# Score matmuls of causal cross-attention, 128 keys at a time, issued as four column groups of 32 keys

## What is computed

```python
def _L0_xattn_ref(x, mem, Wq, Wkv, Wout, bout):
    q = x @ Wq
    kv = jnp.concatenate((mem, x), axis=1) @ Wkv
    k, v = jnp.split(kv, 2, axis=-1)
    q, k, v = (to_heads(q), to_heads(k), to_heads(v))      # 16 heads of 16
    dots = jnp.einsum('bhid,bhjd->bhij', q, k) * scale
    mask = j_idx > i_idx + mem_len                          # causal, memory always seen
    dots = jnp.where(mask[None, None], -jnp.inf, dots)
    attn = jax.nn.softmax(dots, axis=-1)
    out = jnp.einsum('bhij,bhjd->bhid', attn, v)
    ...
    return out @ Wout + bout
x = x + _L0_xattn_ref(_layernorm(x, axis=-1), ctx_1024, ...)
x = x + _L0_ffn_ref(_layernorm(x, axis=-1), Wg, W1, W2)    # 8 experts, one per token
```

## Time and profile before

| | |
|---|---|
| median of 3 runs | 507.42 us (505.65 to 510.08) |
| the profiled execution's own time | 509.3 us |
| its span, first to last instruction | 507.5 us |
| mean granted TensorE clock over the span | 0.925 |
| PE busy | 391.2 us, 77% |
| ACT busy | 262.1 us, 52% |
| DVE busy | 234.8 us, 46% |
| attention part of the span | 113.7 to 316 us |

### The profile page before, as it was taken

The page is one execution under the profiler, slowest core; times in us unless marked ns, Lnnn a source line. Parts: engine busy times, 40 slices in busy tenths (PEclk is TensorE's granted clock), DMA queues, the critical chain, the costliest instruction groups (busy, mean ns, idle before and its releaser), DMA issues.

```text
span 507.5 us, 8833 instructions
## 1 busy us (share of the span) xinstructions
PE 391.2 (77%) x2753; PEld 229.3 (45%) x2756; DVE 234.8 (46%) x858; ACT 262.1 (52%) x361; POOL 104.9 (21%) x154
## 2 busy tenths in 40 slices
PE   0386984479999997999799998889511689989994
PEld 0332741263332422332233332767400688878883
DVE  6967782422343523443343443888688830011111
ACT  1133342238999895999589997322400025444440
POOL 8513850410000000000000000000000033555552
PEclk9999899698999997999899999999655599999998
DMA  8004572387040404040404700024200021222220
GB/s 281 3 31 133 160 219 86 104 275 255 3 135 4 135 1 134 0 134 1 135 0 120 223 2 1 0 84 163 87 1 0 1 57 51 85 68 80 68 64 31
DMA packets 30254, 43.32 MB, mean 85 GB/s; under 512 B 5166, under 2 KB 18096, under 8 KB 30208
## 3 DMA queue, kind: packets, MB, share of 16 engines
q1 hardware_dynamic: 27536, 36.17, 22.5%
q0 software_dynamic: 2672, 6.61, 4.3%
HBM read 30.76 MB, written 13.58 MB: 87 GB/s over the span
## 4 chain that ended last, share of the span: by engine, by line
PE 52%; DVE 22%; ACT 11%; issue 10%; DMA 3%; POOL 1%; DVEq 1%; POOLq 0%; ACTq 0%; SPq 0%
PE ps L828 17%; PE ps L812 10%; ACT pbuf L667 9%; PE ps L987 7%; PE ps L997 7%; PE ps L784 3%; DVE pbuf L1066 3%; DVE v_st L1292 3%; PE ps L913 2%; DMA k_cut<-piece 1%; DVE pbuf L1158 1%; DVE n L1125 1%; DVE nt L1063 1%; PE ps L929 1%; PE ps L793 1%
## 5 line engine op out<-in xcount | busy, mean ns | idle before, releaser
L667 ACT ACTIVATE pbuf<-ps 128x1024 f32<-128x1024 f32 (+3 forms) x192 | 173.2, 990 | 28.9 <-PE ps L812 28.9
L1202 DVE SCALAR_TENSOR_TENSOR pbuf<-pbuf,seen 128x128 f32<-128x128 f32 (+2 forms) x288 | 68.1, 275 | 104.7 <-ACT pbuf L667 104.7
L812 PE MATMUL ps<-q_st,k_st 98*128 98x512 bf16 (+4 forms) x512 | 99.4, 326 | 13.9 <-ACT pbuf L667 11.2
L828 PE MATMUL ps<-pbuf,v_st 128*32 128x512 f32 (+4 forms) x1024 | 91.6, 487 | 7.0 <-DVE mid L1208 5.5
L812 PEld LDWEIGHTS ps<-q_st,k_st 98*128 98x128 bf16 x512 | 39.6, 99 | 83.1 <-ACT pbuf L667 45.3
L828 PEld LDWEIGHTS ps<-pbuf,v_st 128*32 128x32 f32 x1024 | 27.1, 110 | 56.2 <-issue 32.0
L1393 DVE SCALAR_TENSOR_TENSOR mid<-ps,slot_gate,mid 128x256 f32<-128x256 f32 x20 | 9.7, 484 | 81.3 <-PE ps L997 81.3
L704 ACT COPY piece<-wts 128x1024 f32 x20 | 20.9, 1047 | 48.4 <-DVE more L1380 45.1
L997 PE MATMUL ps<-wts,mid 128*128 x160 | 38.9, 387 | 5.1 <-ACT mid L714 3.4
L987 PE MATMUL ps<-mid,piece 128*128 128x128 f32 x320 | 39.1, 275 | 1.2 <-issue 1.2
L987 PEld LDWEIGHTS ps<-mid,piece 128*128 128x128 f32 x320 | 38.7, 192 | 2.6 <-issue 1.7
(11 more groups left out here) (203 smaller groups left out, 450.8 us busy)
## 6 DMA issues: line engine op xcount, KB each, us to landing
wts<-in_L_ffn_W SPq DMA_DIRECT2D x16, 512.0 KB, 8.5
k_st<-k_cut SPq DMA_DIRECT2D x48, 147.2 KB, 2.9
q_st<-q_cut SPq DMA_DIRECT2D x48, 128.0 KB, 2.7
token_rows<-pbuf SPq DMA_DIRECT2D x4, 1024.0 KB, 4.3
q_cut<-piece SPq DMA_DIRECT2D x8, 384.0 KB, 2.6
k_cut<-piece SPq DMA_DIRECT2D x8, 384.0 KB, 3.0
xres<-in_x SPq DMA_DIRECT2D x4, 512.0 KB, 6.4
pbuf<-in_L_xattn_Wkv SPq DMA_DIRECT2D x1, 512.0 KB, 7.2
```

Source lines behind the costliest of these rows:

```text
L667: nc.scalar.activation(pbuf[:, s % 2, r, c0:c1], st_ps[(s * GH + r) % NST][:, c0:c1], ACT.Exp, scale=SCALE).then_inc(exp_done, 1)
L812: last = nc.tensor.matmul(st_ps[(s * GH + r) % NST][:, a:z], k_st[pa][:, r, t * P:(t + 1) * P], q_st[pa][:, r, q0 + a - c0:q0 + z - c0], s ...
L828: last = nc.tensor.matmul(o_ps[32 * r:32 * r + 32, a:z], v_st[pa][:, t, r, :], pbuf[:, s % 2, r, a + dc:z + dc], start=(t == 0), stop=(t = ...
L1202: last = nc.vector.scalar_tensor_tensor(a, a, 3.0e38, seen[:, off:off + w], ALU.min, ALU.mult)
```

## The change

Every score matmul with 128 keys becomes four with 32 keys each. They have the same moving operand; the weights are 32 keys of `k_st`, and the output is 32 partitions of the same PSUM columns, so each of the four lies in another group of 32 columns of the array, as the four heads' value matmuls do. Semaphores stay as they were: the first of the pieces waits, the last signals.

```diff
             for (t, q0, c0) in STEPS[s]:
                 for (a, z) in split_at_bank(c0, c0 + S - q0):
-                    last = nc.tensor.matmul(st_ps[(s * GH + r) % NST][:, a:z], k_st[pa][:, r, t * P:(t + 1) * P],
-                                            q_st[pa][:, r, q0 + a - c0:q0 + z - c0], start=True, stop=True)
+                    for c in range(0, P, 32):
+                        last = nc.tensor.matmul(st_ps[(s * GH + r) % NST][c:c + 32, a:z],
+                                                k_st[pa][:, r, t * P + c:t * P + c + 32],
+                                                q_st[pa][:, r, q0 + a - c0:q0 + z - c0], start=True, stop=True,
+                                                skip_group_check=True)
             last.then_inc(st_ready, 1)
```

## The result

The changed kernel takes 521.36 us (median of 4 runs, 515.62 to 522.47) against 507.02 us before on the same chip: a ratio of 1.024, 95% interval 1.019 to 1.029. It is slower, by 1.9 to 2.9%. The profiled execution took 520.75 us, with a span of 518.8 us at a mean clock of 0.91. In what follows a time is the median of all executions of a kernel, while a ratio to the kernel before leaves out those that ran in the slower state.

A forecast was written before the change was run, and what follows sets the result against it. The bound was attention's wait chain of PE's scores and values and ACT's exp. Switches saved 6.3 us, narrow pieces cost 0.3, instruction waits 2.0: 4.0 us less, 503.4 against 507.42. Range 500.3 to 511; the case's own 500.5 to 507.

The forecast's parts named there:

- Switches: Between value and score matmuls of a step: gaps of 0.10 and 0.095 us vanish, 6.3 us, 6.0 after narrow pieces.
- C: The gap belongs to type together with tile, or quads cost what they save: 509.4 us, or 507.4; chance 0.10.
- D: Score quads of 512 columns take 0.43 us, on the path in heads 2 and 3: 539 us; chance 0.07.
- Does the body stay?: PE's loop body grows from about 1390 to 2160 instructions and is no longer kept: 503.4 us, otherwise 501.4.
- the term of 2.0 us: At PE's two jumps back: a 4.3 us wait for instructions, mostly covered, adds 0.8 to 1.0 us a turn.
- 3.5 us of cover: At the loop's turn: PE's step 5 values end 3.5 us before DVE's copy needs them, hiding that much waiting.
- a sign of being wrong: The turns of PE's loop get longer by more than the steps get shorter; no size given.
- Rival B: PE's wait at the jump back and branch outgrows its cover: at 8 us of waiting 510.4 us; chance 0.14.
- a term put at nothing: PE's branch over the unused maxima block: waiting counted only right behind the jumps back, none at other group entries.
- Clock: Around the loop's turns: the fall to 1.2 GHz shifts by up to 1.9 us a turn either way; taken as 0.

The follow-up runs named there:

- the two kernels without the block: The kernel before without the skipped maxima block in PE's loop: 506.11 us; the changed kernel, all scores in quads, without it: 499.97 us.
- the runs with 64 keys: Changed kernel with each score matmul as two of 64 keys instead of four of 32, body 1652 instructions: 522.86 us, ratio 1.031 to the kernel before.
- body of 2164: The kernel before with 384 small matmuls, never executed, added in PE's skipped maxima blocks, body 2164 instructions: 519.33 us, ratio 1.023.
- the kernel with the rolled maxima: Changed kernel with the branched-over maxima block written as a PE loop over the heads, body 1820 instructions: 507.12 us, ratio 0.999 to the kernel before.
- the kernel without the block: Changed kernel with the branched-over maxima block replaced by one small matmul, body 1620 instructions: 499.97 us, ratio 0.984 to the kernel before.
- the two with heads 2 and 3 in quads: Changed kernel with only heads 2 and 3 split in four: with maxima rolled into a loop 500.81 us, with maxima as they were 512.36 us.
- 280 dummies: The kernel before with 280 small matmuls, never executed, added in PE's skipped maxima blocks, body 1956 instructions: 539.19 us, ratio 1.064.

## Why the prediction was wrong

**Switches.** Right: 6.0 us forecast for attention, 6.1 us measured where the body stays (196.5 against 202.6, and again 6.1 between the medians of the two kernels without the block). A steady group is 22.96 us; the 23.1 to 23.2 foreseen was counted down from 24.0, and from the 23.88 that a group really took it is 0.92 us less, where 0.885 had been forecast. The gap belongs to the tile's width, as the runs with 64 keys show, and quads of bfloat16 stream at the full rate; rivals C and D are out.

**Does the body stay?** Right in its outcome, that it doesn't, but by an argument that was too simple. I took the length of the body, 2160 instructions, as what decides. A body of 2164 can stay and one of 1652 can't.

**The wait after the jump back.** This is the step that failed, the term of 2.0 us. I had read 4.3 us off DVE and set 3.5 us of cover against it. The cover was about right: with a wait of 4.5 us, in the kernel with the rolled maxima, 1.1 to 2.0 us a turn come through, and 0.8 to 1.0 were forecast. The wait was wrong. PE stands still for 7.04 us at the first turn and 7.74 us at the second, since the branch behind the jump misses as well: 3.6 us for the jump and 3.9 us for the branch, then 4.5 and 3.6 us. The two turns, each with the group behind it, take 55.3 and 57.0 us, against 51.2 and 51.2 with a body that stays: 4.1 and 5.8 us, 9.8 together where 2.0 were forecast. The waits less 3.5 us of cover would give 3.5 and 4.2; the branches at the entries of the fifth and the seventh group, 1.6 us each, lie in the same stretches. The turns did get longer by more than the steps got shorter, which the prediction had named as a sign of being wrong. Rival B had this mechanism and its size, 4.5 us a turn at 8 us of waiting. I gave it 0.14 because the branches of the kernel before cost no visible time; that spoke only of a body whose blocks were at hand.

**The other entries of a group.** This is the second half of the same failure, a term put at nothing, and no rival had it. The same branch stands at each of the eight groups, and I counted it only at the turns. It takes 3.4, 1.8 and 2.9 us at the entries of the second, the third and the last group, and scores stand right behind it, for which ACT waits. The chain shows the first as

```profile
135.05 0.95 ACT pbuf L667
136.00 2.01 issue
138.01 1.93 PE ps L813 x24
```

and from one group's first exp to the next's, over these entries, it is 27.26, 25.64 and 24.92 us instead of 22.90, 22.96 and 22.96 in the kernel without the block: 4.4 + 2.7 + 2.0 = 9.0 us. Part of it is the clock: from 138.9 to 142.3 us PE runs at 0.50.

**The sum again.** 507.5 us of span - 6.1 (quads) + 9.8 (turns) + 9.0 (other entries) - 3.3 (head of the program) + 1.9 (tail) = 518.8, which is the span. That it closes proves nothing, since all terms are read from three profiled executions; what it gives is the sizes. The first three terms are set apart by experiments: where 2.0 us of waiting for instructions were forecast, it is 18.8. That the turns and entries cost by the block in the queue and not by what is executed is shown by two pairs of kernels: the changed kernel with and without it, and the two with heads 2 and 3 in quads, which differ in 344 instructions never executed. In both pairs the blocks on q8 and the long branches come and go together with the time. Head and tail I can't explain: the first exp starts between 108.6 and 115.1 us in these kernels with no order in it, and the tail, from the start of the last copy, lasts 190.0 to 193.3 us.

**Clock.** I had put it into the range with up to 1.9 us a turn. It fell elsewhere, as foreseen: what PE did after its own wait, from 193.4 us on, ran at 0.50, and PE had stood still for 7 us before it. What it costs by itself no run told apart from the wait.

## What to carry to other kernels

Before issuing one instruction as four inside a loop, count the blocks of 256 that a pass touches, code that is branched over included where it shares a block or is read ahead, and keep them within 8 on PE. Past that the whole body was fetched in each pass here; a jump back cost 3.3 to 4.7 us and a branch over 275 instructions or more up to 4.2, which only work already queued on other engines can hide. The prices are those of this kernel. Split only the matmuls that stand next to a change of tile, and roll up code that never runs: here that turned 2.4% slower into 1.2% faster.

## What was not expected of the hardware

- The step is sharp: with 1620 instructions no block is fetched in the second pass, with 1652 nine are.
- Making a skipped stretch longer can help. 280 dummies in skipped code gave 539 us, 384 gave 519, and where the shorter skip brings 10 blocks in each pass, the longer brings none.
- A branch costs by the length of what it skips when the body isn't kept: 103 or 193 instructions 0.2 to 0.4 us inside the loop, 275 anything from 0.3 to 4.1 us, 547 or more 3.5 to 4.2 us. What decides within the middle case, I take to be where the branch stands in its block and how much time the read-ahead had; that wasn't tried.
- Four bfloat16 matmuls in four column groups take 0.22 us for 512 columns, as long as one matmul of the full width.
